# A layer normalisation moved from ahead of the first attention group into it, on VectorE

## The reference

```python
x = _layernorm(x + _L0_attn_ref(x, ...), axis=-1)   # a gated linear recurrence
x = _layernorm(x + _L0_ffn_ref(x, ...), axis=-1)    # 64 experts, top 8, and shared experts
x = _layernorm(x + _L1_attn_ref(x, ...), axis=-1)   # attention, 16 heads of 8
x = _layernorm(x + _L1_ffn_ref(x, ...), axis=-1)    # three layers of +1/-1 weights
```

## Time and profile before

| | us |
|---|---|
| median of 3 runs | 694.94 |
| lowest and highest | 692.66, 695.42 |
| the profiled execution, its own time | 692.66 |
| its span, first to last instruction | 690.4 |

### The profile page before, as it was taken

One profiled execution on the slowest core, in us unless ns is written; L12 is line 12 of the kernel. 1 busy time (PEld: TensorE's weight loads), 2 busy tenths in 40 slices (PEclk: granted clock), 3 DMA queues, 4 the chain that ended last, 5 costly groups with the idle time before them and its releaser, 6 DMA issues.

```text
span 690.4 us, 12448 instructions
## 1 busy us (share of the span) xinstructions
PE 548.4 (79%) x3438; PEld 343.6 (50%) x3471; DVE 486.5 (70%) x1125; ACT 376.8 (55%) x844; POOL 397.9 (58%) x420
## 2 busy tenths in 40 slices
PE   3940880007999999999886899799989999888995
PEld 2330660006999999999773223233323333434553
DVE  5489696003666656777688788679878887669886
ACT  3310330002666666666758577576767777877541
POOL 7330678777777704776687877787839000225652
PEclk9975695556999999999999799989999999999998
DMA  5999771115777867888674334215303110000001
GB/s 179 385 392 273 261 245 46 53 49 175 225 225 220 226 176 201 219 229 221 165 205 138 81 109 118 67 42 151 101 2 117 50 37 1 2 1 0 16 16 31
DMA packets 101862, 94.08 MB, mean 136 GB/s; under 512 B 11015, under 2 KB 86887, under 8 KB 101607
## 3 DMA queue, kind: packets, MB, share of 16 engines
q1 hardware_dynamic: 93630, 76.81, 36.9%
q0 software_dynamic: 8192, 16.79, 8.7%
HBM read 45.92 MB, written 47.19 MB: 135 GB/s over the span
## 4 chain that ended last, share of the span: by engine, by line
PE 42%; POOL 25%; DVE 13%; issue 12%; DMA 4%; ACT 3%; SPq 0%; POOLq 0%; DVEq 0%
PE ps L1393 11%; POOL xd L505 9%; PE ps L1380 8%; POOL arena L517 5%; PE ps L1403 4%; PE ps L1388 4%; DVE mx L1091 3%; PE ps L1497 3%; PE ps L1507 3%; PE ps L1487 3%; POOL arena L531 2%; POOL big L517 2%; DVE arena L1209 2%; DVE st L811 2%; POOL arena L529 2%
## 5 line engine op out<-in xcount | busy, mean ns | idle before, releaser
L1091 DVE TENSOR_REDUCE mx<-ps 128x2 f32<-128x1024 f32 x128 | 150.8, 1217 | 31.5 <-PE ps L1487 30.8
L714 ACT ACTIVATE big<-ps 128x512 f32<-128x512 f32 x256 | 141.3, 598 | 49.5 <-PE ps L1497 41.6
L505 POOL DMA_INDIRECT xd<-xt,idx x128 | 131.2, 1025 | 62.0 <-issue 62.0
L517 POOL DMA_INDIRECT big<-od,idx x80 | 79.4, 993 | 49.9 <-DMA od<-big 24.9
L1393 PE MATMUL ps<-arena,xbT 128*128 x512 | 99.7, 318 | 0.0
L1403 PE MATMUL ps<-idf,big 128*128 128x128 f32 x256 | 49.9, 278 | 54.2 <-DMA big<-xd 54.2
L1013 DVE TENSOR_TENSOR hm<-sg,ps 128x176 f32<-128x176 f32 x128 | 43.1, 337 | 64.9 <-ACT sg L653 64.3
L1497 PE MATMUL ps<-arena 128*128 128x512 bf16 (+1 forms) x234 | 81.3, 394 | 7.8 <-ACT big L714 4.7
L1017 DVE COPY xbT<-ps 128x256 f32<-128x256 f32 x128 | 53.5, 418 | 45.1 <-PE ps L1403 44.9
L653 ACT ACTIVATE sg<-ps 128x176 f32<-128x176 f32 x128 | 40.6, 317 | 80.6 <-PE ps L1393 76.2
L1487 PE MATMUL ps<-arena 125*128 125x512 bf16 (+1 forms) x256 | 71.9, 394 | 15.3 <-DVE mx L1091 13.3
(11 more groups left out here) (215 smaller groups left out, 871.8 us busy)
## 6 DMA issues: line engine op xcount, KB each, us to landing
xd<-zeros SPq DMA_DIRECT2D x2, 8192.0 KB, 45.1
big<-xd SPq DMA_DIRECT2D x64, 256.0 KB
od<-big SPq DMA_DIRECT2D x64, 256.0 KB
arena<-scr SPq DMA_DIRECT2D x96, 96.0 KB
arena<-w_gu SPq DMA_DIRECT2D x1, 5632.0 KB
scr<-places SPq DMA_DIRECT2D x8, 384.0 KB, 3.1
arena<-w_d SPq DMA_DIRECT2D x1, 2816.0 KB
xd<-xt,idx POOLq DMA_INDIRECT x128, 2.2
```

Of the source, the lines that this page charges most:

```text
L505: pool.indirect_dma_start(out=xd[f], out_offset=bass.IndirectOffsetOnAxis(ap=idx[:, t, k:k + 1], axis=0), in_=xt[:, t], in_offset=None).th ...
L517: pool.indirect_dma_start(out=slot[:, k], out_offset=None, in_=od[f], in_offset=bass.IndirectOffsetOnAxis(ap=idx[:, t, k:k + 1], axis=0)). ...
L714: act.activation(ering[:, HG * (mt % 2) + h], ps[:, 4 + h % 2, :], ACT.Exp, scale=SCALE).then_inc(exp_ready, 1)
L1091: v.tensor_reduce(mx[:, k, TB * h + 2 * a:TB * h + 2 * a + 2], ps[:, 2 * a:2 * a + 2, :], AX_X, ALU.max).then_inc(s1_free, 1)
```

## The change

The normalisation of sequence 1 is no longer issued at L1174 but in `dve_group(0, 0)`, behind the row maxima `(2, h=0, a=0)` and `(2, h=0, a=1)` and `copy_max(1, 1)`. Nothing else is changed; the instructions, their number and their operands are the same.

```diff
@@ -1140,7 +1140,7 @@ dve_group
-                            if (h, a) == (0, 1) and i in TURN_IN and i:
+                            if (h, a) == (0, 1) and i in TURN_IN:
                                 normalise(xt, tmp, 2 * B + TURN_IN[i])
@@ -1171,7 +1171,6 @@
             for step in range(4):
                 split_max(1, 1, step)
-            normalise(xt, tmp, 2 * B + TURN_IN[0])
             for i in range(HEAD_GROUPS):
                 dve_group(i, i % 2)
```

## The result

| | before | after |
|---|---|---|
| median of 12 runs, us | 694.2 | 698.9 |
| lowest and highest | 691.35, 698.21 | 692.05, 702.06 |
| span of the profiled execution | 690.4 | 695.7 |

The ratio after to before is 1.0065, 95% interval 1.0041 to 1.0091. The four statistics of the second normalisation cut the span into stretches whose ends have one meaning in every kernel: the times at which DVE begins them. A difference ahead of the first mark used here, the statistics of sequence 1, can't come from group 0.

What follows compares the result with a forecast made beforehand. POOL's chain was taken to bound 380.42 to 503.14 us. 692.66 + 0 (old place) + 0 (delay inside the slack) + 0.6 (POOL) = 693.3 us, as a median 695.5; range 691.5 to 699.0.

Steps and rivals of the forecast that it cites:

- likeliest case: Delay hidden in DVE's slack before the statistics of sequence 2, only POOL's own delay reaches the end: +0.6 us, chance 0.58.
- rival 2: At PE's turning of sequence 1, the wait lowers PE's clock and the delay exceeds 3.58 us: +2.4 to +4.0, chance 0.12.
- Rival 3: Groups 4 to 7 shift against POOL, shortening its 18.68 us period: -2.4 us, up to -3.4, chance 0.11.
- What was taken away is worth nothing: At the old place, 386.64 us, removing four `tensor_scalar` (1.27 us) only lengthens DVE's idle time to about 2.2: gain 0.
- rival 4: Taking 1.27 us off DVE ahead of group 0 starts the groups and the end earlier: -1.3 us, chance 0.07.
- The four instructions take turns with POOL's sum: In the new place, from about 391.3 us, the four stretch to some 5 us and PE turns sequence 1 2.9 late.
- POOL is delayed by 0.6 us: POOL's additions beside the new place lose some 0.2 us to each of three DVE turns: 0.6, bounds 0 and 1.4.
- 2.9 us is less than 3.58, so from the delay itself 0 reaches the end: DVE's idle 3.58 us before the statistics of sequence 2 absorbs the 2.9 us delay, leaving about 0.7 idle: 0.
- Rival 1: PE's low clock at 446.5 to 453.5 us vanishes, but the clock falls behind 503 us: +2.2 us, chance 0.12.
- two ways to count the old place: POOL's DMA issue at the old place: by the profile row 0.04 us given back, by the skill's rule up to 1.1.

Runs made afterwards that it cites:

- POOL waits: The changed kernel, but POOL waits for the normalisation of sequence 1 before the weighted sum beside it; ratio to the kernel before 1.0038.
- Delay without lock: The kernel before, normalisation in its old place, but its signal to PE given in the changed place by the last of eight constant reductions; ratio 1.0083.
- PE kept busy: The changed kernel with three extra matmuls that PE executes ahead of its wait for the normalisation, result overwritten; ratio to the kernel before 1.0073.

## Why the prediction was right in its range and wrong in its likeliest case

The measured time lies within the range, 0.1 us below its upper end. That is luck: the range reached up there only because it went half-way into rivals 2 and 3. The likeliest case, +0.6 us and within 0.5%, did not come; rival 2 did, which had 0.12.

- **What was taken away is worth nothing:** right. The idle time behind the old place became 2.24 us, forecast 2.2, and rival 4 is refuted.
- **The four instructions take turns with POOL's sum:** right. They took 4.83 us, forecast about 5, and PE turned 2.8 us late (396.89 - 393.49, less the 0.64 from ahead; its wait was 3.19), forecast 2.9. That it is POOL's sum that lengthens them there is shown by the kernel in which POOL waits (1.10 us). One detail was wrong: the first of the four, begun 0.17 us ahead of POOL's multiplication, did not get through but took 2.17 us.
- **POOL is delayed by 0.6 us:** wrong. Its first three additions took 2.60 us, before 2.61. The four short instructions waited for POOL and held up none of its; the 512-column ones at the second sum did (3.29 against 2.95 us), though. POOL came to the statistics of sequence 2 0.9 us later, which did not show behind DVE's delay.
- **"2.9 us is less than 3.58, so from the delay itself 0 reaches the end":** this step failed. It took the lag as constant over 50 us. It grew from 2.8 us (the first step) to 8.6 (9.3 less the 0.64 from ahead): 1.5 behind the first low clock, 2.9 through DVE instructions pushed beside POOL's second sum (1.8 net of before's own collision), 2.3 behind a second low clock, which followed PE's wait for just these instructions, and 0.3 more. Of the 8.6 the idle time of 3.58 absorbed its part, and 5.1 reached the statistics of sequence 2. I had read the row that shows such a collision (1.78 us at 408.62) and used it as a measure of the lock, not as a neighbour that a lag of some us would push more instructions against. "Delay without lock" shows that the delay by itself is enough (71.0 us), "POOL waits" that without the lock it does not arise (67.2), and "PE kept busy" that a lag of 2.8 us, below the slack, still ended in a loss of 4.7. How the growth divides between the second sum and the clock behind it is read from the timelines and is not separated by an experiment.
- **Rival 2** named the right place and the clock, and its point of decision (a lag beyond 3.58 us) is what the trace shows at the statistics; but it priced one low stretch of 11 us at 2.5, where two of 3.4 us came with steps of 1.5 and 2.3, and it lacked the second sum. Its +2.4 to +4.0 stood against 5.3 in the span and 4.7 in the medians.
- **Rival 1:** half of it came. The low clock of 446.5 to 453.5 is gone in the changed kernel, but groups 4 to 7 gained only 0.3 us (58.1 for 58.4), since POOL ends them; nothing was lost behind 503 (187.2 both). In the changed kernel's second profile a low clock did stand there, from 512.7 to 516.1 us, and the stretch took 187.8. It comes and goes in the same kernel: with a low clock between 505 and 518 us the last stretch took 187.5 to 188.5 us (six profiles), without one 186.9 to 187.2 (seven).
- **Rival 3** did not come: POOL's period in group 4 was 481.94 - 463.53 = 18.41 us, before 18.68, so 0.3 of its 3.0 us.
- **The Trainium skill**, page SBUF — State Buffer, section Who interferes with whom, states that `tensor_reduce` never contends with GpSimd on this chip; the reductions beside the first sum agree, 0.6 us each. Of the two ways to count the old place, the row's 0.04 us is not contradicted: POOL's multiplication began 12.82 us behind the statistics of sequence 1 before (391.56 - 378.74) and 12.80 after (392.08 - 379.28), so no more than this was given back, and not up to 1.1 us.

## What to carry to other kernels

Before an instruction is moved on an engine, look at what the engine with which it takes turns executes in the new place, and at what everything behind it will stand beside once it is late. Slack that is read at one meeting point is slack for a lag that stays as it is; where lagging work falls beside another engine's sums, or PE's wait lowers its clock, 1 us can become 4, or in the next execution nothing. One profile does not price such a place, and an edit that is to hold an engine up has to be looked up in the trace: here one wait held up nothing. A move within a tightly interleaved group is priced by the whole group's phase, not by the gap into which it fits.

## What was not expected of the hardware

- Beside a run of POOL arithmetic, four `tensor_scalar` of 128x128 took 2.17, 1.40, 0.88 and 0.61 us instead of about 0.34, each until 0.07 to 0.09 us behind the end of POOL's instruction, and POOL's were not lengthened (1.91 and 2.60 us).
- A 0.69 us `tensor_tensor` that began 0.1 us ahead of POOL's multiplication still took 2.56 us.
- The same wait of PE can leave its clock alone or not: behind 2.31 us at the turning it stayed full, behind 2.23 us at the same place in another profile it was at the lower level for 3.4 us, which added 1.5 us to the lag.
